# Full-array products ahead of every layer-1 score bank, and maxima rows sent before half the queries

## What is computed

```python
x = x + _L0_xattn_ref(ctx, _layernorm(x), ...)     # 16 heads of 64, the context attends to x and itself
x = x + _L0_ffn_ref(_layernorm(x), ...)            # 8 experts of width 1024, top 2
x = x + _L1_xattn_ref(_layernorm(x), ctx, ctx, ...)
x = x + _L1_ffn_ref(_layernorm(x), ...)            # 4 gated experts, identities, a causal convolution
```

```python
q = (queries @ Wq.T + bq).reshape(N, L, H, -1)     # N = 2, L = 1024, H = 16 heads of D = 16
k = (keys @ Wk.T + bk).reshape(N, S, H, -1)        # S = 77 context rows
sm = einsum('nlhd,nshd->nlhs', q, k) / sqrt(D)     # then a causal mask: key s only for row l >= s
attn = einsum('nlhs,nshd->nlhd', softmax(sm), v)
out = attn.reshape(N, L, H * D) @ Wo.T + bo
```

## Time and profile before

| | us |
|---|---|
| median of 3 runs | 1827.38 |
| lowest and highest | 1818.76, 1833.07 |
| the profiled execution | 1823.52 |
| its span | 1821.8 |
| TensorE busy | 1562.2 (86%) |
| VectorE busy | 1237.7 (68%) |
| GpSimd busy | 898.0 (49%) |
| ScalarE busy | 705.7 (39%) |

### The profile page before, as it was taken

One profiled execution on the slowest core, in us unless ns is written; L12 is line 12 of the kernel. 1 busy time (PEld: TensorE's weight loads), 2 busy tenths in 40 slices (PEclk: granted clock), 3 DMA queues, 4 the chain that ended last, 5 costly groups with the idle time before them and its releaser, 6 DMA issues.

```text
span 1821.8 us, 44029 instructions
## 1 busy us (share of the span) xinstructions
PE 1562.2 (86%) x18034; PEld 1282.3 (70%) x18034; DVE 1237.7 (68%) x2503; ACT 705.7 (39%) x1312; POOL 898.0 (49%) x862
## 2 busy tenths in 40 slices
PE   1899999999998999999999973499989855898798
PEld 0677777787777777877787752488888743566587
DVE  8757777777777678777777765244478666555765
ACT  1434544454444444444444431244534514222122
POOL 3246555665563365566565651576555616221322
PEclk9999999999999999999999986799999965655699
DMA  9134433442432253335334301799999781700001
GB/s 215 37 72 114 105 83 94 106 117 75 102 93 63 69 123 77 95 94 127 90 85 106 102 36 54 289 407 406 402 385 397 267 156 12 116 3 1 35 12 35
DMA packets 92973, 239.39 MB, mean 131 GB/s; under 512 B 17611, under 2 KB 40707, under 8 KB 92388
## 3 DMA queue, kind: packets, MB, share of 16 engines
q1 hardware_dynamic: 89028, 226.32, 43.0%
q0 software_dynamic: 3744, 10.26, 1.5%
HBM read 144.31 MB, written 39.72 MB: 101 GB/s over the span
## 4 chain that ended last, share of the span: by engine, by line
PE 53%; DVE 15%; DMA 13%; POOL 8%; issue 5%; ACT 2%; SPq 0%; DVEq 0%; ACTq 0%; POOLq 0%
PE ps L1916 21%; PE ps L2015 9%; DMA xs<-xslots 8%; PE ps L1949 5%; PE ps L1995 5%; PE ps L1996 5%; DMA latf<-wexp 4%; POOL PR L864 3%; DVE PR L1415 3%; POOL wst L876 2%; PE ps L2182 2%; DVE mxs L1349 2%; PE ps L2274 2%; DMA QS<-NM 1%; DVE wtmp L1443 1%
## 5 line engine op out<-in xcount | busy, mean ns | idle before, releaser
L864 POOL TENSOR_TENSOR PR<-PT 128x512 f16<-128x512 f32 (+1 forms) x416 | 441.2, 1070 | 421.7 <-ACT PT L1088 421.0
L1088 ACT ACTIVATE PT<-ps 128x512 f32<-128x512 f32 (+1 forms) x576 | 323.8, 596 | 366.0 <-PE ps L1996 365.8
L2015 PE MATMUL ps<-V_h,PT 128*128 128x65 f16 (+1 forms) x2304 | 324.9, 197 | 26.5 <-DVE PR L1415 20.7
L2015 PE MATMUL ps<-V_l,PT 128*128 128x65 f16 (+1 forms) x2304 | 320.4, 195 | 0.0
L2015 PE MATMUL ps<-V_l,PR 128*128 128x65 f16 (+1 forms) x2304 | 318.7, 194 | 0.0
L2015 PE MATMUL ps<-V_h,PR 128*128 128x65 f16 (+1 forms) x2304 | 318.2, 194 | 0.0
L2015 PEld LDWEIGHTS ps<-V_h,PT 128*128 128x128 bf16 (+1 forms) x2304 | 226.9, 98 | 121.2 <-issue 48.6
L1349 DVE TENSOR_REDUCE mxs<-ps 128x1 f32<-128x736 f32 x256 | 235.3, 919 | 48.3 <-PE ps L1949 48.3
L1995 PE MATMUL ps<-QA,KA 128*128 128x512 f32 (+1 forms) x576 | 247.8, 430 | 5.8 <-DMA QB<-maxT 5.2
L1996 PE MATMUL ps<-QB,KB 65*128 65x512 f32 (+1 forms) x576 | 231.0, 401 | 0.0
L2015 PEld LDWEIGHTS ps<-V_l,PT 128*128 128x128 bf16 (+1 forms) x2304 | 228.9, 99 | 0.7
(11 more groups left out here) (351 smaller groups left out, 3645.6 us busy)
## 6 DMA issues: line engine op xcount, KB each, us to landing
wx<-wsplit SPq DMA_DIRECT2D x46, 2048.0 KB, 11.4
QA<-Q_h SPq DMA_DIRECT2D x64, 256.0 KB, 4.6
latf<-wexp SPq DMA_DIRECT2D x32, 512.0 KB, 4.3
wsplit<-wst SPq DMA_DIRECT2D x32, 512.0 KB, 2.9
KA<-K_h SPq DMA_DIRECT2D x32, 275.5 KB, 3.1
KA<-K_l SPq DMA_DIRECT2D x32, 275.5 KB, 4.0
KB<-K_h SPq DMA_DIRECT2D x32, 275.5 KB, 5.4
QB<-Q_l SPq DMA_DIRECT2D x32, 256.0 KB, 5.5
```

The lines of the kernel that those rows point to most:

```text
L864: nc.gpsimd.tensor_tensor(PR[0:m, s % RING, :], PT[0:m, s % RING, :], upper(s)[0:m], ALU.subtract).then_inc(s_rem_pool, 1)
L1088: nc.scalar.activation(PT[0:m, s % RING, :], score_banks[s % 2][0:m], ACT.Exp, scale=HD ** -0.5).then_inc(s_exp, 1)
L2015: mm = nc.tensor.matmul(pv_bank[:, q, :], p, v, start=(kt == 0 and q == 0 and k == 0), stop=(kt == KT - 1 and k == 3), skip_group_check=True)
```

## The change

1. Each `scores1(k)` issues, after its waits and before its score, two products of 128 rows, 128 columns and 512 moving columns into the score's own bank (ten at k = 4, 12, 20 and so on, every eighth). Their results are not used: the score overwrites the partitions that are read.
2. 16 such products stand between `max1_rows` of batch 0 and the first score.
3. SP sends the maxima rows ahead of the queries of half c = 1: for batch 0 all three transfers of that half come after both maxima rows, for batch 1 the transfers of the second four heads of c = 1.
4. The remainders of half heads 5 and 7 go from VectorE to GpSimd.

```diff
-        R1V = [k for k in range(1, K1S, 2) if 4 <= k < 12 or (12 <= k < 32 and k % 4 == 3) or k >= 32]
+        R1V = [k for k in range(1, K1S, 2) if 8 <= k < 12 or (12 <= k < 32 and k % 4 == 3) or k >= 32]
+        FULL0 = 16
@@ sync, batch 0
-            for c in range(NC):
-                stack_queries1(0, c, 0)
+            stack_queries1(0, 0, 0)
             sp.wait_ge(s_a1e, NM_JOB[0] + 2)
             for c in range(NC):
                 stack_max1(0, c, 0)
+            stack_queries1(0, 1, 0)
             stack_keys1(1)
@@ sync, batch 1
             sp.wait_ge(s_sc1, 2 * (HC + 4))
-            for c in range(NC):
-                stack_queries1(1, c, 1)
+            stack_queries1(1, 0, 1)
             sp.wait_ge(s_a1e, NM_JOB[1] + 2)
             for i in range(2):
                 for c in range(NC):
                     stack_max1(1, c, i)
+            stack_queries1(1, 1, 1)
@@ tensor
+            def full_product(k):
+                nc.tensor.matmul(ps[:, 3 + k % 2, :], wa["h"][:, 3, 0, 0:P], flat(wa["h"][:, 0]), start=True, stop=True)
+
             def scores1(k):
...
                 slot = j if b == 0 else (HC + j) % QSLOTS
                 r = slice(HD * c, HD * c + QROWS)
+                for i in range(10 if k % 8 == 4 else 2):
+                    full_product(k)
                 mm = nc.tensor.matmul(o, KS[r, b, j, 0:S], QS[r, slot, HALF * a:HALF * a + HALF], start=True, stop=(a == 1))
...
                 max1_rows(0, half)
+            for i in range(FULL0):
+                full_product(0)
             for k in range(AHEAD):
                 scores1(k)
```

## The result

| | before | after |
|---|---|---|
| median in the comparison, us | 1830.22 | 1851.02 |
| lowest and highest | 1818.76, 1835.01 | 1847.56, 1853.63 |
| the profiled execution, its span | 1823.52, 1821.8 | 1847.56, 1845.8 |
| mean granted clock | 0.904 | 0.921 |

The ratio is 1.0127, with a 95% interval of 1.0094 to 1.016: the change costs 1.3%, although the mean granted clock went up. The forecast was 1841, with 1812 to 1868 as its range; the time lies in it, 10 us above the point.

The account below looks back on a forecast made before the run. Successive limits bound layer-1 attention: a wait for rows, VectorE and GpSimd, projections and maxima, then TensorE, busy at 1.2 GHz. Terms -8 + 1.5 + 5 + 5 + 11.5 - 1 = +14 gave 1841 us on the median's scale, range 1812 to 1868.

Parts of the forecast that it names:

- 1 start: Up to VectorE's first normalisation: earlier maxima rows gain 11 us, products ahead cost 3; -8 us.
- 2 VectorE and GpSimd: Normalisation chain to the second transposed group: moved remainders and a late exponential cost little; +1.5 us.
- 3 half heads 14 to 19: Stretch with the projections: five pairs and one ten added, the ten raising the clock first; +5 us.
- 4 batch 1's maxima: Half heads 20 to 27: added products only partly hidden under reductions, middle between both clock levels; +5 us.
- 5 half heads 28 to 63: TensorE-bound stretch: +3 us at 2.4 GHz, +45 at 1.2 GHz, mostly at the upper level; +11.5 us.
- 6 tail: Last two groups' projections: the first gains up to 4 us if the level is still high; -1 us taken.
- the four fifths: Half heads 28 to 63: share taken at the upper clock level, giving 3 + 42/5 = +11.5 us.
- rival (c): Half heads 28 to 63: level lost soon after each ten, one third at 2.4 GHz; total +42, 1869 us; chance 0.22.
- The mechanism of the level: TensorE's clock: what it is busy with decides, since a fully busy stretch had 0.50; no size of its own.
- The rule of the Trainium skill: TensorE's clock gate answers to how busy it is; by its letter full products change no level; small chance.

Follow-up runs that it names:

- e1: Kernel before with only the order of SyncE's transfers changed, no full products, remainders as before; ratio 0.9953 to the kernel before.
- e6: Changed kernel with only the 16 full products ahead of the first score, none in `scores1`; ratio 0.9947 to the kernel before.
- e8: Changed kernel, 113-row batch-1 scores, only twelve full products ahead of half head 32 and one before each batch-1 score; ratio 0.9854 to the kernel before.
- e11: Changed kernel with twelve more full products ahead of batch 1's first score, in the wait for its maxima rows; ratio 1.0022 to the kernel before.
- e3: Changed kernel with 49 rows instead of 128 in each of the 208 added products; ratio 1.035 to the kernel before.
- e2: Changed kernel with transfer order and remainders as before, all 208 full products kept; ratio 1.0196 to the kernel before.
- e4: Changed kernel with three full products ahead of each score instead of two, still ten at every eighth; ratio 1.0119 to the kernel before.
- e5: Changed kernel without the pairs, keeping the 16 products at the start and ten at every eighth score; ratio 1.0025 to the kernel before.
- e9: e8 with batch 1's scores at 49 rows again; ratio 1.0027 to the kernel before.
- e7: Changed kernel with batch 1's scores contracting over 113 rows instead of 49, the added rows meeting zeros; ratio 0.999 to the kernel before.
- e10: e8 without the one full product ahead of each batch-1 score; ratio 0.9903 to the kernel before.

## Why the prediction was off by 10 us, step by step

The parts, as the prediction numbered them, from the two chains:

| part | predicted | measured | from |
|---|---|---|---|
| 1 start | -8 | -9.7 | 1512.85 to 1503.16 |
| 2 VectorE and GpSimd | +1.5 | +1.3 | 1545.62 to 1537.22 |
| 3 half heads 14 to 19 | +5 | +3.1 | first reduction of batch 1's maxima, 1562.24 to 1556.99 |
| 4 batch 1's maxima | +5 | +4.1 | 1592.45 to 1591.29 |
| 5 half heads 28 to 63 | +11.5 | +26.7 | 1666.66 to 1692.18 |
| 6 tail | -1 | -1.5 | the rest of the spans |
| sum | +14 | +24 | |

Part 5 was put 15.2 us too low and the other five together 5.2 too high, so that a third of the miss was cancelled. The closeness of the total is to that extent luck; without it the time would have been near 1856, still in the range.

**Parts 1 to 4 and 6** came out within 2 us each. Some of that closeness is luck too: the writing of the maxima rows, ahead of the change, came 4 us and more later in other executions (e1). The first score was put at 1496 and started at 1495.6, in an execution that wrote the rows as early as the one before; in e6, e8 and e11, which wrote them later, it started between 1499.3 and 1500.0. e1 and e6, with 0.9953 and 0.9947, show that the whole gain is the order's. The end of the first half went as worked out, batch 1's maxima with the level coming and going: it was at 1.00 in 1583 to 1584 and at 0.50 in 1585 to 1586.

**Part 5 failed, in one term: the four fifths.** Both ends of the sum were right. At the full clock the products cost 67.9 - 65.1 = +2.8 us (e11) where I had +3 (in detail not all of it: an output projection took 2.98 and 3.13 us in e8, not 2.65); without it +42.7 (e3) where I had +45. With 49-row products a half head is 0.11 us cheaper than with 128-row ones (last section); with that counted, e3 gives an estimate of 42.7 + 32 x 0.11 = +46. A plain half head takes 1.43 us at 2.4 GHz where I had 1.45, as TensorE's timeline of the changed kernel shows:

```profile
1672.89 0.45 PE L2280 MATMUL ps<-QS,KS 49*77 49x512 f32 x1
...
1674.32 0.46 PE L2280 MATMUL ps<-QS,KS 49*77 49x512 f32 x1
```

But the share at the upper level was not four fifths: the mean granted clock of 0.67 is (0.67 - 0.50) / 0.50 = one third of the time, some 31 of 92.9 us. At the pace of e11, 67.9 us for the whole stretch, as much time does 0.46 of the work. The formula takes a share of the work; with 0.46 it gives 3 + 42 x 0.54 = +26, and +26.7 was measured. By time or by work the share lies under the two thirds at which the prediction said that rival (c) decides: at its place (c) held, to which I had given 0.22. The total stayed at +24, and not at (c)'s +42, mainly because (c) also made the other parts dearer, and those held.

Why the share was wrong: I wrote "a lost clock lasts for less than one such round; the stage starts it low after the 3.8 us wait", and so knew of the low start but took each burst of ten to end it. A burst does so only sometimes. In the stretch from first to last score, ten bursts of the changed kernel, e2, e4 and e5 began at the lower level; seven were followed by a rise before their end or within 1 us of it, three were not (half head 36 in the changed kernel and in e4, half head 44 in e5). In the changed kernel the level first rose at 1619, 24 us after the first score. Of the 61 us that this stretch spent at 1.2 GHz, that is 24; the other 37 came after the level had been up, in three falls (below). In e11, with the level up at the first score, neither came, and the same instructions took 25 us less. That a wait filled ahead of the stretch saves most of the loss is shown by the two ratios; that the later falls, too, come of the low start is not, since e2 also started low (13 us) and then lost the level only once, for 3 us.

**The mechanism of the level** was half right. That it counts what TensorE is busy with, and not only that it is busy, stands firmly: e3 against the changed kernel (0.50 and 0.67), e9 against e8 (0.53 and 1.00). The rule of the Trainium skill that was weighed there (TensorE: Matmul & The Clock Gate, Part 1 and closing table) would have given all four the upper level; TensorE was busy for all of the 107.8 us of e3 and the 81.4 of e9, and the measurements decide against it.

**What stays open.** In the changed kernel the level, once up, was lost three times in the loop, near 1622, 1643 and 1650, with the same two products for each half head that kept it for 68 us in e11 and for over three quarters of the stretch in e2 ((0.89 - 0.50) / 0.50). Stretches of 1 us of the changed kernel show the rise and the three falls (the last value but two is the mean clock of the microsecond in which it changed):

```profile
1619.00:1620.00 1.00, 1.00 (x20) 0.82 (x19) 0.21 (x1) 0.59 (x1) 0.00 (x0) 1.00 0.00 0
...
1622.00:1623.00 1.00, 1.00 (x20) 0.95 (x20) 0.21 (x1) 0.60 (x1) 0.00 (x0) 0.69 0.00 0
...
1642.00:1643.00 1.00, 1.00 (x19) 0.75 (x20) 1.00 (x4) 0.37 (x1) 0.00 (x0) 0.93 0.07 16
...
1649.00:1650.00 1.00, 1.00 (x19) 0.78 (x19) 1.00 (x2) 0.59 (x1) 0.68 (x1) 0.85 0.00 0
```

Two of the falls come as an output projection begins (1622.33 in the chain above), which then runs its 4.92 us at 1.2 GHz, and the third as eight transposes begin. Nor do the rises go by the tens alone: those at 1639 and 1666 come with half heads 44 and 52, those at 1619 and 1646 some 3 us after a set of eight transposes began and with no burst near. I did not find what tells these stretches from the others. The traces would fit that two products to a 49-row score lie at an edge, and three (e4) or 113 rows (e7) on its safe side; each of these rests on one execution. Why a burst misses or hits is not settled either.

## What to carry to other kernels

The place of products added to hold TensorE's level told more here than their number: twelve in a wait of 3 us ahead of a dense stretch were worth 1% (1.0127 to 1.0022), while a third one for each half head changed nothing that can be told from noise (1.0119), and the pairs without the twelve cost 1% (e5 against the changed kernel). Before adding any, look at the rows of the products that are there: with the scores' rows filled against zeros, the variant with one product each was 1.5% faster than the kernel before, and with the rows left at 49 it was 0.3% slower. And when a clock level is a term of the sum, price both levels from rows, as was done, but let the state at the start of the stretch last until something that the trace has shown to raise it from that mixture, and take such a rise as a chance and not as certain when it is seen only sometimes.

## What the hardware showed that was not expected

A half head costs less when its score fills more rows. From one chain piece to the next at 2.4 GHz, the pair, a 49-row score and the value products take 0.56 + 0.38 + 0.49 = 1.43 us (changed kernel, from 1672.39), and with a 113-row score 0.56 + 0.23 + 0.40 = 1.19 (e7, above). At 1.2 GHz and without added products it is 1.17 with 49 rows and 0.98 with 113 (e10). The number of columns is the same each time. It is also cheaper, by less, when the added products have the score's 49 rows. The chain of waits of the changed kernel, one half head at 1.2 GHz (2.22 us):

```profile
1608.93 1.05 PE ps L2263 x2
1609.98 0.64 PE ps L2280
1610.62 0.53 PE ps L1917 x16
```

and that of e3 (2.11 us):

```profile
1642.92 1.15 PE ps L2264 x2
1644.07 0.43 PE ps L2281
1644.50 0.53 PE ps L1917 x16
```

The chain counts from end to end. By starts the same score takes 0.64 and 0.56 us, so only the sum of the three is sure. All this would fit a price for each change in the number of rows from one product to the next; no run isolates it. In e8 the stretch fell to 50.1 us with as many scores as before.

And rows that meet only zeros counted for the granted clock: e8 and e9 differ in them alone among TensorE's products, and ran at 1.00 and 0.53.
